# Last image's grouped 3x3 convolution moved to 32x32 tiles of TensorE

## The reference, cut to what matters

```python
# sizes: base_kernel (8, 32, 32, 3, 3); x (4, 256, 64, 64)
w[g] = rotate(base_kernel[g], angle[b, g])             # 32 x 32 x 3 x 3
y[g] = conv3x3(group_norm(x)[b, g], w[g], padding=1)   # 32 channels in, 32 out
x[b] = x[b] + gate[b] * y
```

## Time and profile before

| what | value |
|---|---|
| median of 3 runs | 7217.41 us |
| the profiled execution | 7214.56 us, of which 7212.8 us from the first to the last instruction |
| mean granted TensorE clock | 0.753 of full speed |
| L1's matmuls of the last image | 127 us, from 6499.5 us on |

### The profile page before, as it was taken

The page is one execution under the profiler, slowest core; times in us unless marked ns, Lnnn a source line. Parts: engine busy times, 40 slices in busy tenths (PEclk is TensorE's granted clock), DMA queues, the critical chain, the costliest instruction groups (busy, mean ns, idle before and its releaser), DMA issues.

```text
span 7212.8 us, 44764 instructions
## 1 busy us (share of the span) xinstructions
PE 3788.9 (53%) x10560; PEld 1992.8 (28%) x10560; DVE 5180.5 (72%) x4868; ACT 1071.3 (15%) x1619; POOL 4557.7 (63%) x4676
## 2 busy tenths in 40 slices
PE   7142241351574526543764256427655652588958
PEld 4121121220222214322321134213223431234533
DVE  5779788796778659856877689757777975432546
ACT  2110000101111002211110022111101210120334
POOL 0777777777777777777777777777777777200000
PEclk9576575675787768766877678768878876799979
DMA  3453544644444333374433333554433355210057
GB/s 106 147 154 104 188 139 137 187 119 156 138 127 127 108 108 123 126 245 145 127 127 106 108 116 130 194 189 127 127 117 108 126 182 182 79 35 32 35 175 186
DMA packets 547456, 954.02 MB, mean 132 GB/s; under 512 B 284448, under 2 KB 349984, under 8 KB 531616
## 3 DMA queue, kind: packets, MB, share of 16 engines
q0 software_dynamic: 221184, 604.27, 26.9%
q1 hardware_dynamic: 326176, 348.65, 14.9%
HBM read 792.21 MB, written 160.37 MB: 132 GB/s over the span
## 4 chain that ended last, share of the span: by engine, by line
POOL 43%; issue 22%; DVE 14%; PE 13%; DMA 4%; ACT 2%; SPq 1%; DVEq 1%; POOLq 0%; ACTq 0%
POOL ring L378 43%; PE PS L699 12%; DVE ring L1355 5%; DVE dbuf L1361 3%; DMA img<-d_dram 2%; DMA ring<-table,idx_stage 1%; ACT img L1068 1%; DVE sm L1771 1%; DVE sm L1794 0%; DVE sm L1787 0%; DVE stats L1885 0%; DVE img L1798 0%; PE PS L796 0%; DMA img<-q_dram 0%; DVE wb_sb L1805 0%
## 5 line engine op out<-in xcount | busy, mean ns | idle before, releaser
L378 POOL DMA_INDIRECT ring<-table,idx_stage x4608 | 4539.8, 985 | 1439.1 <-issue 1365.4
L1361 DVE TENSOR_REDUCE dbuf<-ring 128x64 f32<-128x2304 f32 x512 | 2070.7, 4044 | 31.8 <-DMA d_dram<-dbuf 3.8
L699 PE MATMUL PS<-img,wb_sb 128*128 128x512 f32 (+1 forms) x3328 | 1621.6, 647 | 437.4 <-DVE img L1649 280.6
L699 PE MATMUL PS<-img,wa_sb 128*128 (+1 forms) x1984 | 926.1, 628 | 592.7 <-DVE img L1745 225.1
L1355 DVE TENSOR_TENSOR ring<-ring,wt 128x576 f32<-128x576 f32 x1216 | 838.9, 751 | 431.8 <-DMA ring<-table,idx_stage 321.0
L699 PEld LDWEIGHTS PS<-img,wb_sb 128*128 128x128 f32 x3328 | 684.1, 209 | 1341.6 <-issue 1047.9
L1355 DVE TENSOR_TENSOR ring<-ring,PS 128x2304 f32<-128x2304 f32 x208 | 530.5, 2551 | 368.0 <-DMA ring<-table,idx_stage 364.3
L699 PEld LDWEIGHTS PS<-img,wa_sb 128*128 128x128 f32 x1984 | 395.9, 202 | 1093.4 <-issue 1033.1
L699 PE MATMUL PS<-sm,params 128*128 128x4 f32 (+1 forms) x32 | 9.1, 355 | 792.5 <-DVE sm L1399 729.7
L796 PE MATMUL PS<-params,img 128*128 128x128 f32 x256 | 62.9, 427 | 678.8 <-DMA img<-d_dram 677.6
L699 PE MATMUL PS<-wa_sb,cb 128*128 128x108 f32 (+1 forms) x1024 | 238.9, 399 | 335.5 <-DVE cb L1420 335.5
(11 more groups left out here) (196 smaller groups left out, 3196.8 us busy)
## 6 DMA issues: line engine op xcount, KB each, us to landing
ring<-table,idx_stage POOLq DMA_INDIRECT x4608
table<-cb SPq DMA_DIRECT2D x64, 512.0 KB, 6.1
img<-y_dram SPq DMA_DIRECT2D x64, 512.0 KB, 6.6
q_dram<-img SPq DMA_DIRECT2D x32, 1024.0 KB, 4.2
img<-q_dram SPq DMA_DIRECT2D x32, 1024.0 KB, 7.2
img<-in_x SPq DMA_DIRECT2D x8, 2048.0 KB, 12.1
y_dram<-cb SPq DMA_DIRECT2D x64, 256.0 KB, 2.3
d_dram<-dbuf SPq DMA_DIRECT2D x128, 128.0 KB
```

The costliest lines, as they stand in the source:

```text
L378: nc.gpsimd.indirect_dma_start(out=ring[:, g, p * CORNERS * GC:(p + 1) * CORNERS * GC], out_offset=None, in_=tab[b], in_offset=bass.Indire ...
L699: return nc.tensor.matmul(o, l, r, start=start, stop=stop, **kw)
L1361: vec.tensor_reduce(dbuf[:, j, g * GC:(g + 1) * GC], ring[:, g, :].rearrange("p (k c) -> p c k", c=GC), AX_X, ALU.add).then_inc(sem("ring_ ...
```

## The change

For the last image alone (`b == B - 1`), L1's main part runs in four stages of straight code, one for each quad (chunks 0 to 3, chunks 4 to 7) and half k. In a stage PE issues, for each tap, 16 matmuls of 32 rows by 32 columns over 512 pixels: chunk j of the quad and group r use the array's rows `32 r` and its columns `32 ((r + j) % 4)`, so that within a tap the 16 matmuls take the 16 places of the array, one each. Their weights are the diagonal blocks of the same `wa_sb`. The result of chunk j lies in bank `2 * j + k` with its groups turned by j, and no two places write the same 32 partitions of one bank.

On DVE, each stage turns the groups back while it adds: one instruction of 128 partitions for j = 0, four of 32 partitions for j = 1, two of 64 for j = 2 and four of 32 for j = 3, then four bn_stats. `lC` and `lX` count once for each stage. PE waits for DVE in the second quad only, for the stage that read the same four banks.

```diff
+        def packed(n):
+            return START + (B - 1) * CHUNKS + n
...
+                def l1_packed(quad, k):
+                    if quad:
+                        pe.wait_ge(sem("lX"), packed(k + 1))
+                    for tap in range(K2):
+                        for j in range(4):
+                            for r in range(4):
+                                to = (r + j) % 4
+                                at = R_SIZE + (k * K2 + tap) * P + r * CG
+                                rs, os_ = slice(r * CG, (r + 1) * CG), slice(to * CG, (to + 1) * CG)
+                                last = mm(rows(PS[os_, 2 * j + k, :]), wa_sb[rs, at:at + CG],
+                                          padded(k, quad * 4 + j, tap // 3, tap % 3)[rs], tap == 0, tap == K2 - 1,
+                                          tile_position=(r * CG, to * CG), skip_group_check=True)
+                    last.then_inc(sem("lC"), 1)
+
+                if b < B - 1:
+                    loop(l1)
+                else:
+                    for quad in range(2):
+                        for k in range(KC):
+                            l1_packed(quad, k)
...
+                def l1_packed(quad, k):
+                    n = quad * KC + k
+                    dve.wait_ge(sem("lC"), packed(n + 1))
+                    for j in range(4):
+                        img = chunk_of(img1, k, quad * 4 + j)
+                        width = (P, CG, 2 * CG, CG)[j]
+                        for first in range(0, P, width):
+                            to = slice(first, first + width)
+                            at = (first + j * CG) % P
+                            last = vec.scalar_tensor_tensor(out=img[to], in0=PS[at:at + width, 2 * j + k, :],
+                                                            scalar=mod[to, k:k + 1], in1=img[to], op0=ALU.mult, op1=ALU.add)
+                    last.then_inc(sem("lX"), 1)
+                    dve.wait_ge(sem("lX"), packed(n + 1))
+                    for j in range(4):
+                        vec.bn_stats(seg(stats, (quad * 4 + j) * 6 + k * 48, 6), chunk_of(img1, k, quad * 4 + j))
```

More of the change, by code:

```diff
@@ L890, in l1 @@
                         last.then_inc(sem("lC"), 1)
-                loop(l1)
+                def l1_packed(quad, k):
[17 more added lines that the diff above has]
+                            l1_packed(quad, k)
                 barrier()
@@ L1751, in l1 @@
                         stream.give(1, 4)
-                chunks("L1" if gi != B - 1 else "L1 last", gi, 0, l1)
+                def l1_packed(quad, k):
[13 more added lines that the diff above has]
+                        vec.bn_stats(seg(stats, (quad * 4 + j) * 6 + k * 48, 6), chunk_of(img1, k, quad * 4 + j))
+                if b < B - 1:
+                    chunks("L1" if gi != B - 1 else "L1 last", gi, 0, l1)
+                else:
+                    for quad in range(2):
+                        for k in range(KC):
+                            l1_packed(quad, k)
                 barrier()
```

## The result

The changed kernel runs in 7145.48 us (median of 4 runs, 7142.65 to 7147.35) against 7217.44 (median of 4, 7217.14 to 7224.44) on the same chip: ratio 0.9898, 95% interval 0.9881 to 0.9915. It is 72 to 74 us faster where I had forecast 54.6, and lies at the very edge of both my ranges (7145), beyond it by the ratio (0.9898 x 7217.41 = 7143.8). Run again beside the later experiments it gave 7141.44 against 7219.48, ratio 0.9895 (0.9878 to 0.9911; 4 runs against 7).

What follows compares the result with a forecast made beforehand. PE was taken to bound the changed stage (busy 126.86 of 127.00 us). 65.1 - 126.9 + 7.2 = -54.6 us from the 7217.41 us median gave 7163 us, own range 7145 to 7178, 8-in-10 range 7145 to 7355.

Steps and rivals of the forecast that it cites:

- The stage is on the path and nothing beside it takes over: Last image's L1 stage: PE busy 126.86 of 127.00 us, so time PE saves comes off the end until DVE is late.
- A pass takes 0.429 us in a place, and a place runs one at a time: PE's changed stage: each float32 matmul is two passes of 0.429 us in its place, 0.858 us, as before.
- PE 62 us: PE's four changed stages: 144 matmuls a row strip, one 0.429 us step each, 61.8 us; 65 with the clock's start.
- Issue 48 to 75 us: PE's sequencer issuing 576 matmul calls: 75 us at 0.13 us each, 48 at 0.083 without the register instruction.
- The pair pace of 0.055 us as a ceiling: PE's weight loads: 1152 pairs of load and matmul at 0.055 us each, at most 63 us.
- DVE hidden beside PE, 10.0 us a stage: DVE's additions and bn_stats take 10.0 us a stage; the first three stages lie beside PE's later ones of 15.5 us.
- +7.2 us at the end: DVE's last stage, open after PE ends, grows from 2.8 to 10.0 us; +8.1 at worst.
- Strict order: Rival: PE starts matmuls in program order across the whole array; +130.7 us, 7348 us; chance 0.33.
- strips alone: Rival: only the four row strips overlap, columns within one don't; +7.2 us, 7225 us; chance 0.12 shared with low clock.
- no overlap: Rival: PE's places don't run side by side at all; +378 us, 7595 us; chance 0.06.
- The low clock: Rival: PE's granted clock stays at the lower level for the stage; 7225 us; chance 0.12 shared with strips alone.
- Sum: Whole kernel: PE's stage 65.1 in place of 126.9 us, plus 7.2 at the end, -54.6 us, giving 7163 us.

Runs made afterwards that it cites:

- four and eight places: Against the changed kernel: turning undone, 4 of 16 places used, 7228.85 us; groups turned by 0, 1, 0, 1, 8 places used, 7156.76 us.
- 256 pixels: Against the changed kernel, each matmul runs over 256 pixels in place of 512: 7141.41 us; also with 16 weight columns in place of 32: 7154.67 us.
- place by place: Against the changed kernel, only PE's call order changed: all 9 taps of one place, then the next place; 7874.56 us.

## Why the prediction was right or wrong, point by point

- *The stage is on the path and nothing beside it takes over.* Right: every us saved between the first matmul and the last bn_stats came off. L2 and L3 took 573.6 us from L2's first long matmul on, 573.8 before.
- *A pass takes 0.429 us in a place, and a place runs one at a time.* Right: 3.42 and 1.71 us a tap with four and eight places.
- *PE 62 us.* This is the term that failed. I took the step "within a strip each pass waits for the pass before it in its own place", so that only two calls overlap in a strip. The 16 first passes that start within 0.1 us show that a second pass waiting for its place doesn't hold up the other places. PE needed 41.6 us: the array's own 30.9, which stood in my list as a bound and which I set aside because of the issue bounds of 48 and 75, some 5.8 for 36 taps at 1.02 in place of 0.858, 3 for the low clock of the first 6 us, 1.1 of waiting for DVE and 0.6 for the last pass's own length.
- *Issue 48 to 75 us.* Wrong. Both came from the register instruction's pace at the start of the stage before. With 256 pixels PE took a call in 0.60 / 16 = 38 ns (at most 58 with the gaps); the subtraction gave 83. So the 0.13 us a call that I read there wasn't the cost of issuing four instructions and 46 ns more; what it was the runs don't show.
- *The pair pace of 0.055 us as a ceiling.* Right as a ceiling, 63 us, and far from the 0.019 us of the run with 256 pixels.
- *DVE hidden beside PE, 10.0 us a stage.* The size was nearly right (10.9, since pieces that start at another partition cost 0.76 and not 0.66). That it would be hidden hung on PE's 15.5 us a stage, and fell with it (9.2 us). The sentence on what happens when PE is faster held: DVE became the bound, with 43.6 us behind a first PE stage of 12.6.
- *+7.2 us at the end.* +11.5: DVE was 3.6 us behind when PE ended, beside its own last stage.
- *Strict order (0.33), strips alone, no overlap.* None held. The low clock was a real danger, but not here: the last image's stage had 0.50 for its first microseconds, then 1.00, as before; place by place it never rose.
- *Sum.* PE gave 23.5 us more than forecast and the open end 4.3 less: 54.6 + 23.5 - 4.3 = 73.8.

By the Trainium skill ("TensorE: Matmul & The Clock Gate", section "Measured speedup vs the span model") 16 places give 10.6 times, from which I had 47 us as an estimate. The runs show 16 x 0.858 / 1.02 = 13.5 times for a tap in a steady stream of float32 passes, and 494 / 41.6 = 11.9 for PE's whole part with its start and its wait; the measurement decides.

## What to carry to other kernels

A block-diagonal float32 matmul wastes the array, and giving each diagonal block a place of its own pays only if the blocks of several outputs are turned so that all places are used; call them round-robin, one call a place, never all calls of a place in a row (729 us slower here). When one engine gets three times as fast, redo the sum for its consumer first: here evacuation and not TensorE set the time, and a share for an idle engine took the next 9 to 10 us off the stage. A list of bounds of a rate is only as good as the row that each comes from; the bound that came from a different mix of instructions (with register work) deserved the least weight.

## What the runs showed of the hardware that I had not expected

- A second pass that waits for its place doesn't hold up other places: 15 of them waited when the sixteenth place started. But with all passes of a place in a row, the next place starts only when four of the place before are left.
- The granted clock stayed at 0.50 for 776 us of unbroken matmuls with about 1.3 places at work, and was 1.00 with four.
- An addition on DVE that starts at another partition than the one before costs about 0.1 us more, and a narrow one that doesn't costs nothing more (1.51 and 1.40 us for two, one pair a stage).
- Straight code may have a price of its own: in the second stage of the runs with 256 pixels PE idles for 0.42 to 1.05 us before and behind each 128 passes, released by nothing that the profile shows, and the instruction queue q8 carried 46 packets in place of 38 in all kernels with the straight code. At 1.02 us a tap no such gap shows. That the two belong together is not shown.
